# Two orders changed in a fused four-layer kernel: twelve reciprocal-root steps on VectorE, and the scatters of the expert loops on GpSimd

## The reference

```
x = x + L0_attn(layernorm(x))   # causal attention, 16 heads of 8, 4 key/value heads, rotary
x = x + L0_ffn (layernorm(x))   # 8 experts 128 -> 512 -> 128 with GELU, 2 per row, a shared path, a layer norm
x = x + L1_attn(layernorm(x))   # linear attention by segments of 32 rows, with retrieval of earlier segments
x = x + L1_ffn (layernorm(x))   # 8 experts 128 -> 512 -> 128 with ReLU, 2 per row
_layernorm(x) = (x - mean) / sqrt(var + 1e-5)
```

## Time and profile before

| | |
|---|---|
| median of three executions | 641.87 us (632.91 to 645.01) |
| the profiled execution | 632.19 us |
| its span, first to last instruction | 630.5 us |
| mean granted TensorE clock in it | 0.837 |
| PE busy | 509.7 us (81% of the span) |
| DVE busy | 409.7 us (65%) |
| ACT busy | 293.1 us (46%) |
| POOL busy | 268.2 us (43%) |

### The profile page before, as it was taken

How to read it: one execution, slowest core, us unless ns; L and a number is a source line. 1 busy time by engine, 2 the same in 40 slices (tenths; PEclk the granted TensorE clock), 3 DMA queues, 4 the chain that set the end, 5 groups by cost and what they waited for, 6 DMA issues and landing times.

```text
span 630.5 us, 14217 instructions
## 1 busy us (share of the span) xinstructions
PE 509.7 (81%) x4416; PEld 409.7 (65%) x4416; DVE 409.7 (65%) x1351; ACT 293.1 (46%) x824; POOL 268.2 (43%) x358
## 2 busy tenths in 40 slices
PE   4789998999976699995066999989889684999990
PEld 3565765666544599995055767767677364989990
DVE  5778689687877664633877657756875867453333
ACT  2224553354552466765325366625444321667650
POOL 3324343336476356547000233313543645465550
PEclk9979899596997699998566779977796855999995
DMA  7998000000001222221999000000000002223216
GB/s 231 313 303 327 2 2 1 1 1 23 14 25 39 70 70 83 70 61 48 373 308 346 6 2 2 2 1 2 19 18 3 22 23 57 70 72 84 69 39 208
DMA packets 28376, 53.72 MB, mean 85 GB/s; under 512 B 4816, under 2 KB 24208, under 8 KB 27248
## 3 DMA queue, kind: packets, MB, share of 16 engines
q1 hardware_dynamic: 23216, 42.17, 21.2%
q0 software_dynamic: 4544, 9.45, 4.2%
q10 hardware_dynamic: 544, 1.20, 0.6%
HBM read 42.32 MB, written 29.81 MB: 114 GB/s over the span
## 4 chain that ended last, share of the span: by engine, by line
PE 58%; DVE 26%; issue 5%; DMA 4%; ACT 2%; POOL 2%; SPq 1%; ACTq 0%; DVEq 0%; POOLq 0%
PE ps L1989 12%; PE ps L1997 11%; DVE negm L859 4%; PE ps L2089 3%; DVE X L1362 2%; PE ps L2049 2%; PE ps L1835 2%; DMA w<-ybuf 2%; PE ps L1871 2%; PE ps L1845 2%; PE ps L2073 2%; PE ps L1980 2%; PE ps L1905 1%; PE ps L1770 1%; PE ps L1906 1%
## 5 line engine op out<-in xcount | busy, mean ns | idle before, releaser
L1569 ACT ACTIVATE probs<-ps,w1s 128x128 f32<-128x128 f32 x312 | 89.3, 370 | 48.5 <-PE ps L1989 48.3
L748 POOL DMA_INDIRECT ybuf<-yt,xg x78 | 76.8, 985 | 71.6 <-DVE yt L1116 64.3
L1989 PE MATMUL ps<-xgT,w1s 128*128 128x128 f32 x624 | 87.5, 286 | 2.3 <-ACT xgT L1560 2.1
L1989 PEld LDWEIGHTS ps<-xgT,w1s 128*128 128x128 f32 x624 | 80.1, 201 | 3.4 <-ACT xgT L1560 2.8
L1997 PE MATMUL ps<-w,probs 128*128 x624 | 82.3, 276 | 0.0
L769 POOL TENSOR_SCALAR_AFFINE_SELECT probs<-probs 128x512 f32<-128x512 f32 x64 | 39.2, 637 | 96.5 <-ACT probs L1670 96.4
L859 DVE TENSOR_REDUCE negm<-ps 128x2 f32<-128x512 f32 (+1 forms) x96 | 60.3, 685 | 25.1 <-PE ps L1822 19.4
L1997 PEld LDWEIGHTS ps<-w,probs 128*128 128x128 f32 x624 | 75.7, 192 | 0.1
L694 POOL DMA_INDIRECT xbuf<-rsc,sloti x64 | 62.4, 976 | 30.7 <-DVE sloti L988 15.2
L1483 ACT ACTIVATE probs<-ps 128x512 f32<-128x512 f32 x96 | 51.3, 601 | 35.3 <-PE ps L1845 34.6
L639 POOL TENSOR_SCALAR_AFFINE_SELECT probs<-probs 128x512 f32<-128x512 f32 x64 | 39.2, 637 | 65.4 <-ACT probs L1483 65.2
(11 more groups left out here) (280 smaller groups left out, 1129.0 us busy)
## 6 DMA issues: line engine op xcount, KB each, us to landing
xbuf<-in_c_pads SPq DMA_DIRECT2D x16, 1122.0 KB, 19.0
xg<-xbuf SPq DMA_DIRECT2D x78, 66.0 KB, 1.9
w<-in_w SPq DMA_DIRECT2D x2, 2064.0 KB, 34.0
w<-in_w SPq DMA_DIRECT2D x2, 2048.0 KB, 36.0
w<-ybuf SPq DMA_DIRECT2D x8, 512.0 KB, 5.7
ybuf<-yt,xg POOLq DMA_INDIRECT x78, 2.3
probs<-in_c_sel ACTq DMA_DIRECT2D x2, 512.0 KB, 5.5
bias<-in_b SPq DMA_DIRECT2D x2, 512.0 KB, 31.5
```

The lines of the kernel that those rows point to most:

```text
L748: pool.indirect_dma_start(out=ybuf[l][:, :], out_offset=bass.IndirectOffsetOnAxis(ap=xg[n % AHEAD][:, D:D + 1].bitcast(I32), axis=0), in_= ...
L1569: ins = act.activation(hidT[n % 3][:, c * P:(c + 1) * P], ps[:, q, c * P:(c + 1) * P], ACT.Gelu if l == 0 else ACT.Relu, bias=w[:, FF + c: ...
L1989: mm = pe.matmul(ps[:, n % 2, c * P:(c + 1) * P], w[:, c * P:(c + 1) * P], xgT[n % 2][:], start=True, stop=True)
```

## The change

It has two parts. On DVE, `rstd0` of the last twelve tiles is called at step (-1, 0), right behind their moments, and no longer at step (-1, 3) behind `turn(1)`. On POOL, the loop over the tiles of an expert layer now waits for `y_copied` of tile `n` at the head of turn `n`. In turns 4 to 7 it then sends only one late scatter each, and no results, so that the results are four tiles behind from there on; at turns 12, 16, 20 and 24 it sends two tiles' results, and is level again.

```diff
-LATE_ROWS = 5
+LATE_ROWS = 4
+CAUGHT_UP = (12, 16, 20, 24)
...
             def experts(l):
                 m = ms[l]
                 pair_numbers(l, LATE)
+
+                def scatter_y(n):
+                    pool.wait_ge(gathered[n % AHEAD], loads(l, n))
+                    pool.indirect_dma_start(out=ybuf[l][:, :], out_offset=bass.IndirectOffsetOnAxis(ap=xg[n % AHEAD][:, D:D + 1].bitcast(I32), axis=0),
+                                            in_=yt[n % DEPTH][:], in_offset=None).then_inc(scattered[n % DEPTH], 16)
+
+                behind = 0
                 for n in range(ET):
+                    pool.wait_ge(m["y_copied"], n + 2)
                     if 0 <= n - LATE_ROWS < TOPK * size(LATE):
                         t, k = divmod(n - LATE_ROWS, TOPK)
                         ready_row(l, TILES[LATE][0] + t, LATE)
                         scatter_row(l, TILES[LATE][0] + t, k)
-                    pool.wait_ge(gathered[n % AHEAD], loads(l, n))
-                    pool.wait_ge(m["y_copied"], n + 2)
-                    pool.indirect_dma_start(out=ybuf[l][:, :], out_offset=bass.IndirectOffsetOnAxis(ap=xg[n % AHEAD][:, D:D + 1].bitcast(I32), axis=0),
-                                            in_=yt[n % DEPTH][:], in_offset=None).then_inc(scattered[n % DEPTH], 16)
+                        behind += 1
+                    else:
+                        scatter_y(n - behind)
+                    if n in CAUGHT_UP:
+                        behind -= 1
+                        scatter_y(n - behind)
...
                 if (c, s) == (-1, 0):
                     dve.wait_ge(x_loaded[1], 16)
                     moments0(FIRST, NT)
-                if (c, s) == (-1, 3):
                     rstd0(FIRST, NT)
```

## The result

| | before | with the change |
|---|---|---|
| median | 645.60 us (20 runs, 632.91 to 652.51) | 632.31 us (20 runs, 623.49 to 640.68) |
| profiled execution, its span | 632.19 us, 630.5 us | 632.01 us, 630.1 us |
| mean granted clock in it | 0.837 | 0.854 |

The ratio is 0.986 (0.982 to 0.991). That is a gain of 1.4%, clear of no change but under the 2% from which a kernel is called faster here. In us it is 9 by the ratio, 13 by the medians and 12.1 +- 1.7 by the means (644.8 and 632.7), where 2.2 were forecast. The ratio takes only runs near the fastest of each kernel, and those of before are spread over 20 us, so it shows less than the medians do. To judge single terms I use means over all runs of an experiment beside the ratio; what follows +- is their standard error.

A forecast was written before the change was run, and what follows sets the result against it. PE (58% of the chain) or DVE steps it waits for were taken as the bound. Roots -1.85 and scatters -0.35 summed to -2.2 us, giving 637.7 us, between 635.8 and 639.7; range about 629 to 645.5 us.

The forecast's parts named there:

- The roots' place and price: Prelude: twelve root steps moved behind the moments let `hi` start earlier, -1.85 us, ends at -0.9 and -3.5.
- The upper case of the clock: Prelude: the shorter gap keeps PE's clock up, so the roots' gain could be 3.5 us.
- The shift stays to the end: After the prelude: nothing later runs by absolute time, so the roots' 1.85 us last to the end.
- either way alike: Rival, 15%: the clock's stretches fall otherwise after a changed start, adding or saving one: 632.7 or 642.7 us.
- The scatters: Expert loops, turns 4 to 7: less POOL load removes a weight-copy hold, -0.35 us, bounds 0 to -2.1.
- The cover holds, at zero: Expert loops: gathers behind results four tiles late still come in time, 1.9 us left in turns 8 to 11; no cost.
- I cost the catch-up turns at nothing: Catch-up turns: the second successive scatter runs across the next weight copy, which takes its normal 0.43 us; no cost.
- The rival that each catch-up turn holds a weight copy: Rival, 8%: the second scatter blocks DVE's weight copy, 1.9 us over both layers, sum -0.3, 639.6 us.
- The slower rival, the long chain: Rival, 7%: results four tiles behind make gathers 2.7 us late per layer, sum +3.2, 643.1 us.
- the loss of the prelude's shift: Rival, 15%: PE's clock or a later wait gives the prelude's time back; 639.7 us in place of 637.7.
- The anchor: Starting time of the forecast: a middle between 635.8 us (from four executions' mean) and 639.7 us (from the three-run median).

The follow-up runs named there:

- quiet condition: The last four experiments, in which the unchanged kernel beside them took 630.83 and 632.68 us; its loops took 74.9 and 74.5 us.
- held condition: The first eight experiments, unchanged kernel at 644.50 and 646.59 us, where copies of results came well after their matmuls (held signals).
- filled gap: Kernel before plus twelve unused bf16 matmuls on TensorE ahead of its wait for `hi` and `lo`: 644.02 us beside 646.59, ratio 1.005.
- the pacing with early roots: Whole change without postponed results or catch-up turns; late scatters in turns 4 to 7 behind `y_copied`, against the kernel before: 636.84 us, ratio 0.988.
- the scatters alone with one matmul more: Kernel before with only the GpSimd loop changed, plus one extra 0.22 us matmul in TensorE's prelude gap: 629.26 us, ratio 1.000.
- the whole change with one matmul more: Whole change plus one extra 0.22 us matmul in TensorE's prelude gap, against the kernel before: 633.29 us, ratio 0.979; again 625.18 us, ratio 0.997.
- the results behind until the end: Whole change with catch-up turns 32, 34, 36, 38 in place of 12, 16, 20, 24, against the kernel before: 638.88 us, ratio 0.987.

## Why the prediction was right or wrong

**Sign and range held, and the prelude changed as forecast. The size was off: -2.2 us forecast, some -7 in the quiet condition and -12 in the held one.** That the time fell into the range is luck in part. The starting point was taken 5.7 us too low (639.9, and 645.60 was measured), which made up for half of the missing gain; and the range is 16.5 us wide, so that 645.60 - 2.2 = 643.4 would have been in it as well. The steps, in its order:

*The roots' place and price (1.85 us): right there, and too small at the end.* The roots end at 21.96 (forecast 22.09), the hold is gone, `hi` starts at 25.38 (25.5), the gap is 1.39 us and ends at 27.32 (1.3, 27.5). The upper case of the clock came true in kind: the spreading runs at full clock, and the third pair of maxima starts at 30.72, 2.4 us earlier than at 33.12. About 0.4 of this is the clock's, since the filled gap moved that pair by as much with `hi` in its old place.

"The shift stays to the end" was right as far as it can be followed. The first expert-row scatter starts at 136.4 to 143.5 us, mean 139.0, in the eight profiles with early roots; at 141.3 to 146.3, mean 144.7, in the six with late ones. Much of the spread is the clock's. The stretches from the start to that scatter, for pairs with the same mean clock, first roots late and then early (the unchanged kernel's second profile and the pacing with early roots, both 0.93; the scatters alone with one matmul more and the whole change with one matmul more, both 0.88; columns as in the earlier trace rows):

```profile
0.00:141.32 141.32, 118.87 (x956) 80.97 (x960) 108.47 (x262) 57.66 (x120) 56.51 (x86) 0.93 0.39 132
```

```profile
0.00:138.83 138.83, 117.14 (x956) 79.33 (x960) 107.43 (x262) 57.38 (x120) 56.49 (x86) 0.93 0.40 134
```

```profile
0.00:146.23 146.23, 123.36 (x957) 83.25 (x961) 108.39 (x262) 57.70 (x120) 56.49 (x86) 0.88 0.38 127
```

```profile
0.00:143.45 143.45, 123.14 (x957) 83.15 (x961) 108.78 (x262) 57.70 (x120) 56.53 (x86) 0.88 0.39 130
```

In these pairs the early roots are 2.5 and 2.8 us ahead at the same clock. One more profile with early roots and 0.88, that of the results behind until the end, is further ahead (140.62 us). A line through all fourteen profiles, time against time at the lower level, gives 3.5 +- 0.6 us.

The term that was mis-sized is the price of the whole part: -1.85, with ends at -0.9 and -3.5, where 5.0 +- 1.4 us (quiet) and 4.5 +- 1.4 (held) were measured. What it left out is the clock behind the prelude, which a rival put as "either way alike". In the means it is not alike. The time at the lower level is twice (1 - mean clock) times the span. It fell from 202.9 to 186.5 us with the roots alone and from 206.3 to 189.1 with the whole change, in the quiet condition, each by 16 to 17 +- 5 us; it is 6 to 25 us lower than before in every experiment with early roots. Within one kernel, runs with 1 us more of it are 0.26 us longer (slope over all runs of the experiments), so 16 to 17 us would be worth 4.3 of the 5.0. That is an estimate from a correlation, and with the 2.5 to 3.5 us seen at 140 us it adds up to more than the 5.0, so how the 5.0 divide into shift and clock stays open. A single profile can't price the clock. The stretch 100 to 130 us in the kernel before, in its first and its second profile:

```profile
100.00:130.00 30.00, 27.16 (x192) 18.72 (x192) 21.95 (x54) 12.38 (x27) 9.98 (x18) 0.72 0.00 1
```

```profile
100.00:130.00 30.00, 26.20 (x228) 18.56 (x228) 24.30 (x68) 13.92 (x31) 10.97 (x19) 0.94 0.00 1
```

Why an earlier start lowers the mean time at the lower level stays open. The clock in the gap itself is not excluded as a part of it: with the filled gap that time was 201.3 us beside 214.2, 13 +- 8 us less, without a gain clear of the noise.

*The scatters (-0.35 us, bounds 0 to -2.1): right in the quiet condition, far off in the held one.* Quiet, the loops sum to 149.4 us before, 149.3 with the scatters alone and 148.8 with the whole change, and the scatters alone measured 1.1 +- 1.2 us. Held, they sum to 162.9 and 163.6 with the old loops (the two profiles that have them) and to 157.7 to 158.8 with the new: **-5.1 us** between the means (163.25 and 158.1). This term was mis-sized, since its bounds were read from a profile without held signals. What the old order loses in the held condition was not in it: in both layers copies among the tiles 6 to 10, up to 4.7 us behind their matmuls, and in layer 1 a train of small delays behind them, up to fifteen late copies. Four fixed late copies a layer take their place. Layer 1 gains more by it (82.4 and 82.6 us before, 78.6 to 79.4 after) than layer 0 (80.5 and 81.0, 79.0 to 79.5).

*"The cover holds, at zero": right.* TensorE waits for no gather from tile 4 on, neither after nor with 28 turns behind.

*"I cost the catch-up turns at nothing": right in the quiet condition, wrong in the held one*, where TensorE waits 0.75 to 1.08 us behind each. The rival that each catch-up turn holds a weight copy (8%) had the number of places right and the mechanism not: the copies take 0.43 to 0.62 us in these turns, no full block as the Trainium skill has it (SBUF — State Buffer, Who interferes with whom), and what is late comes two turns behind, from TensorE's side. The slower rival, the long chain, did not come in any profile. Nor did the loss of the prelude's shift.

*The anchor.* The forecast time was a middle between two starting points. The kernel before has a median of 645.60 over 20 runs and 630.83 in another session; its profile was of the quiet kind (loops 74.8 and 74.5), and the profile after of the held kind (79.2 and 78.6). The first kernel is faster by its condition by as much as the second by its change, and so the two spans came out alike.

*Still open.* In the held condition the parts alone gave 3.4 +- 1.3 us each and both together 12.1 +- 1.7, 11.8 +- 1.9 and 12.6 +- 2.1. The terms found here (5.0 for the roots, 5.1 for the loops) make 10, and each measured number is within 1.5 of its errors of them. Either the parts alone were a poor draw, or they help each other by a few us; in the quiet condition they add (5.0 + 1.1 beside 7.0 +- 1.4). These sizes rest on the means; the ratios are clear of no change for the whole change and its variants in the held condition (0.979 to 0.988) and for the roots alone in the quiet one (0.994). What holds the signals, and what sets the condition, was not found.

## What to carry to other kernels

Before two profiles are compared, compare a piece that the change leaves alone, or a program with itself in another session: here one and the same program differed by 8 us, and its loops showed where. A work step taken off the front of the critical path shifts what follows, and the time at the lower clock can change with it; price the second by means over a dozen runs, never from one profile, and compare profiles where their mean clock is the same. An order that avoids several slow instructions in succession on a side engine can be worth 5 us in one condition and nothing in another, so read the bounds of such a term from more than one execution.

## What the hardware showed that I had not expected

- In the held condition, ScalarE and VectorE get matmul results 2.4 and 1.7 us after their modelled end, both within 0.2 us, behind indirect scatters of GpSimd in succession; in the quiet one VectorE gets them after 0.14 us, with the same scatters. Each costs TensorE 0.75 to 1.08 us. Behind four in succession it was 3.66 us, and TensorE waited 2.88 us.
- Such a delay can feed itself: two scatters in succession, a late copy, two scatters again, every 4.05 us (575.00, 579.05) instead of 2 x 1.90 us, until tile 35. It was seen in layer 1 alone.
- A whole session of a one-core kernel can be 2.1% faster than another (630.83 and 644.50 us for the same program).
- Twelve steps of 128x12 on VectorE took 3.43 us beside GpSimd's sum and 2.43 us without it (19.53 to 21.96), nearly all of the difference in one instruction (1.15 and 0.17 us).
